# Mixture of experts behind attention: tokens chosen ahead of the last shared expert, twelve pair slots for the weights, two scatters under way

## The chip, the cores and the metric

The kernel is one launch on one core of a Trainium2 chip. The metric is the device time of that launch in microseconds. The kernel before took 1569.04 us in the median of 3 runs (1566.18 to 1572.91).

## The reference

The input x is 8 batches of 512 tokens with 256 features, all in float32. In short:

```python
x = x + layernorm(attention(layernorm(x)))     # 16 query heads of 128 in 4 groups, causal, softmax
h = layernorm(x)                               # 4096 tokens x 256
scores = softmax(h @ gate_w.T)                 # 64 experts
topk_w, topk_idx = top_k(scores, 6)
# each expert takes the first 64 tokens that chose it (CAP = 64), in order of the token's number;
# for these: d = (silu(t @ w_gate[e]) * (t @ w_up[e])) @ w_down[e]     # 256 -> 176 -> 256
# y[token] = sum over its experts of topk_w * d
y = y + (silu(h @ sh_gate.T) * (h @ sh_up.T)) @ sh_down.T              # shared expert, 352 wide
x = x + layernorm(y)
```

An expert never has more than 64 tokens, and most of the 4096 x 6 choices are dropped. What an expert puts out is added to the rows of its tokens; two experts can have a token in common.

## The kernel before, in words

Everything lives in one program with five instruction streams (SP for plain DMAs, POOL, ACT, DVE, PE), tied by semaphores that are written out by hand. The order of the work is fixed in Python loops; nothing is scheduled at run time.

Attention goes head by head through 128 steps (8 batches x 16 heads). Each batch's output projection, norms, router and shared expert are fitted between the heads of the next batch by a table of places. For the last batch there is no next one, so its rest is done after attention: `turn_y`, `turn_x2`, `route`, `turn_mask`, then six pieces of the shared expert's gate and up (`gate_up`, three column blocks for each of two lanes of 256 tokens) and two of its down projection (`shared_down`). In a piece of `gate_up` ACT makes the tanh (L910), DVE two products (L1238, L1248), ACT the high part (L917) and POOL the low part (`gate_low`, L1486); a lane's product buffer is used again only when POOL has read it.

Each expert's tokens are found as the 64 largest of a row of keys (4096 minus the token's number, or zero). `pick` (L1220) takes eight of them with a MAX8 and a MATCH_REPLACE8 on DVE; for the last batch its eight calls stand between and behind the pieces of `gate_up` (L1353 to 1362). DVE then makes two tables, of tokens to gather and of rows to scatter to, PE turns them (L763, L764), and DVE copies them as integers (L1380). An empty place gathers a row of zeros and scatters to a row set apart for it.

The experts are worked off in 32 pairs: expert 2j in partitions 0 to 63, expert 2j+1 in 64 to 127. For a pair, POOL gathers 128 rows of 320 values (the token's features and its 64 router weights) with an indirect DMA (`gather`, L1545), PE turns them (`expert_turn`, L767), ACT copies, PE multiplies with gate and up (`expert_in`, L777), ACT makes the tanh, DVE the products (`expert_act`, L1383), PE turns (`activations_turn`), ACT copies, PE multiplies with down (`expert_out`, L800), ACT copies to a buffer `dsum` (L1015), and POOL adds the 128 rows to the table `ffn_sums` in HBM with an indirect DMA that accumulates (`scatter`, L1552). The table has two copies: the first expert of a pair adds to copy 0, which also has the shared expert's rows, the second to copy 1. So no row is named twice in one scatter. Rows can be named in two scatters that follow each other, so scatter j waits until scatter j-1 has landed (L1554). There are 5 buffers for gathered rows (NX) and 3 for `dsum` (ND). POOL's order is: four gathers, then for each pair gather j+4 and scatter j.

SP loads the weights expert by expert, three DMAs of 176 KB each (L456), into 16 slots; the first 16 experts are loaded at the end of attention and beside the last batch's rest, the others each when the pair that had the slot has been through `expert_out`. Between them SP reads back the rows that the last residual adds (`fx`, L478). When the last scatter has landed (L503), SP loads both copies of the table (`load_sums`), POOL and DVE add them, DVE and POOL make mean and variance, ACT normalises, DVE adds `fx`, SP stores.

The waits around the scatter:

```python
def scatter(j):                                  # L1552
    if j:
        pool.wait_ge(dma_s, 16 * j)              # scatter j-1 has landed
    ...
    pool.wait_ge(d_made, j + 1)
```

Of the kernel before, what the change touches and what calls it, by code (L numbers as in the profile page):

```python
# [14 lines left out]
P = 128  # L15
TOP_K = 6
CAP = 64
# [13 lines left out]
def build(nc, x, wq, bqT, wkv, bkvT, wo, gwT, w_gate, w_up, w_down, sgT, suT, sdT, consts, out):  # L31
# [6 lines left out]
    NE, _, F = w_gate.shape  # L38
# [7 lines left out]
    TRASH = CAP  # L46
# [14 lines left out]
    sum_rows = [sums[a * SUMROWS:a * SUMROWS + NT, :].rearrange("(b i p) e -> b p i e", p=P, i=TT)  # L61
                for a in range(2)]
    out_rows = out.rearrange("b (i p) e -> b p i e", p=P)

    with ExitStack() as ctx:
# [30 lines left out]
        slot_row = place("slot_row", [P, CAP], F32)  # L96
# [52 lines left out]
        NW = 16  # L149
        w_gu, w_dn, w_where = [], [], []  # L150
        for s in range(NW):
            w_gu.append(place(f"w_gu{s}", [P, 2, 2 * F], F32))
            w_dn.append(place(f"w_dn{s}", [P, 2, E], F32))
            w_where.append(at[0])
        assert at[0] <= weights_end

        at[0] = heads_at
        NX, ND = 5, 3
# [5 lines left out]
        atr = [place(f"atr{i}", [P, 2, P], F32) for i in range(2)]  # L164
        dsum = [place(f"dsum{i}", [P, E], F32) for i in range(ND)]
        tok2 = place("tok2", [P, 2 * CAP], F32)
        sct2 = place("sct2", [P, 2 * CAP], F32)
        empty = place("empty", [P, CAP], F32)
# [9 lines left out]
        at[0] = after_experts  # L178
        NFB = 4
# [4 lines left out]
        fb = [place(f"fb{i}", [P, TT, E], F32) for i in range(2)]  # L184
        assert at[0] <= end_at, (at[0], end_at)
        at[0] = work_at
        fb += [place(f"fb{i}", [P, TT, E], F32) for i in range(2, NFB)]
        fx = [place(f"fx{b}", [P, TT, E], F32) for b in range(NB)]

# [5 lines left out]
        def plain(ap):  # L195
# [9 lines left out]
        dma_s, dma_out = sem("dma_s"), sem("dma_out")  # L205
# [21 lines left out]
                                    "act_turned", "atr_made", "down_in", "d_made"))  # L227
        sum_pool, sum_dve, bias_made, final_normed, final_made = (
# [85 lines left out]

        def lane_of(b, k):
            return k if b == LAST else 0
# [68 lines left out]
        def sync_program(sp):  # L385
# [12 lines left out]
            for t, n in ((ident, P), (pe_t, T), (key_row, HT), (slot_row, CAP), (causal[:, T - P:T], P)):  # L398
# [3 lines left out]
            sp.dma_start(bkv_s[:], bkvT).then_inc(dma_const, 16)  # L402
            for n in range(6):
                load_piece(n)
# [22 lines left out]
            def store_ffn(b, k):  # L427
                _, _, taken, u = use("sd", b, k)
                sp.wait_ge(taken, u + 1)
                sp.dma_start(sum_rows[0][b, :, 2 * k:2 * k + 2, :],  # L430
# [40 lines left out]
            for e in range(NW):  # L471
                if w_where[e] > wkv_end:
                    sp.wait_ge(out_in, N)
                load_expert(e)
            sp.wait_ge(out_in, N)
            sp.wait_ge(values_in, 4 * N)
            for b in range(LAST):
                sp.dma_start(fx[b][:], x2_rows[b]).then_inc(dma_x2in, 16)  # L478
# [5 lines left out]
            for j in range(NP):  # L484
                for u in range(2):
                    if 2 * j + u + NW < NE:
                        load_expert(2 * j + u + NW)
                if j == 1:
# [1176 lines left out]
```

## Time and profile before

| | |
|---|---|
| median of 3 runs | 1569.04 us |
| profiled execution | 1569.09 us, span 1567.3 us, mean granted clock share of TensorE 0.939 |
| busy | PE 1369.7 us (87%), DVE 1089.5 (70%), ACT 840.9 (54%), POOL 814.3 (52%) |
| DMA | 95.78 MB, 61 GB/s over the span; 88722 packets of the plain queue, 6144 of POOL's |
| L1559, scatter issue on POOL | 32 times, 1575 ns each, 97.1 us of idle time before them |

The profile's page has the span in 40 slices of 39.2 us. PE shows nines in slices 3 to 31 and between 0 and 7 after that; the DMA row is near zero in the middle and 4 to 9 from slice 32 on. The change concerns that end: from about 1240 us, where the last heads run and the first weights are loaded, to 1567 us. In the rows below, times are microseconds from the span's start unless marked otherwise, and a line number is that of the kernel before.

### The profile page before, as it was taken

Reading aid. Unit: us, or ns where it says so; the run is one execution under the profiler, and the core shown is the slowest. Engines: PE = TensorE matmul, PEld = TensorE weight load, DVE = VectorE, ACT = ScalarE, POOL = GpSimd, SP = SyncE. Lnnn points to the kernel's source line nnn. Section 1 sums busy time; section 2 is a strip of 40 time slices with the busy share of each in tenths; the row PEclk is TensorE's granted clock in tenths of the full one; section 3 lists DMA queues with packets and bytes.
Section 4 is the critical chain, followed back from the end, with each engine's and each line's share of the span. In section 5 each row is a group of like instructions: output and inputs, shape, how many; then the busy total and the mean of one; then the engine's idle time right before and its main releaser. Section 6 shows DMA issues by size and latency. Waiting matters only on the chain.

```text
span 1567.3 us, 25800 instructions
## 1 busy us (share of the span) xinstructions
PE 1369.7 (87%) x8322; PEld 1168.2 (75%) x8322; DVE 1089.5 (70%) x3524; ACT 840.9 (54%) x2267; POOL 814.3 (52%) x1309
## 2 busy tenths in 40 slices
PE   3899999999999999999999999999999936676710
PEld 3788889888988898889888988898889835333310
DVE  4867686888688868887888688868886855111117
ACT  4666665665566566666666666666665611222204
POOL 2555564556454645464556455645564512344446
PEclk9899999999999999999999999999999967788865
DMA  7100000100000010001000100010000481999765
GB/s 271 46 1 1 14 15 9 37 15 15 22 28 10 14 38 22 1 15 38 21 1 15 38 21 1 15 38 21 1 14 25 110 240 52 237 241 239 165 168 170
DMA packets 94997, 95.78 MB, mean 61 GB/s; under 512 B 6065, under 2 KB 87314, under 8 KB 94866
## 3 DMA queue, kind: packets, MB, share of 16 engines
q1 hardware_dynamic: 88722, 84.70, 17.9%
q0 software_dynamic: 6144, 9.44, 3.1%
q8 instruction: 69, 1.13, 0.3%
q14 instruction: 62, 0.51, 0.1%
HBM read 67.78 MB, written 26.35 MB: 60 GB/s over the span
## 4 chain that ended last, share of the span: by engine, by line
PE 59%; DVE 18%; POOL 7%; DMA 6%; issue 6%; ACT 3%; SPq 0%; POOLq 0%; ACTq 0%; DVEq 0%
PE bank_s L520 14%; PE bank_t L520 13%; PE bank_o L520 10%; PE bank_y L520 9%; PE bank_f L520 5%; DMA ffn_sums<-dsum,idx_s 4%; PE bank_s L600 3%; DVE rows L1081 2%; PE bank_t L600 2%; DVE stat L1060 2%; DVE prob L1148 2%; DVE q_sum L1125 2%; PE bank_f L600 1%; DVE o_l L1166 1%; DVE pt_l L1161 1%
## 5 line engine op out<-in xcount | busy, mean ns | idle before, releaser
L1474 POOL TENSOR_TENSOR prob<-prob,rinv 128x512 f32<-128x512 f32 (+3 forms) x512 | 366.6, 724 | 206.3 <-DVE rinv L1155 204.3
L858 ACT ACTIVATE prob<-prob,negmax 128x512 f32<-128x512 f32 (+3 forms) x512 | 285.5, 558 | 87.8 <-DVE negmax L1148 87.1
L1461 POOL TENSOR_TENSOR q_l<-q_sum,q_h 128x128 fp32r<-128x128 f32 (+1 forms) x256 | 185.5, 745 | 144.4 <-ACT q_h L838 143.2
L520 PE MATMUL bank_o<-pt_h,v_h 128*128 128x128 f32 (+3 forms) x512 | 169.4, 331 | 0.0
L520 PE MATMUL bank_o<-pt_h,v_l 128*128 128x128 f32 (+3 forms) x512 | 165.0, 322 | 0.0
L520 PE MATMUL bank_o<-pt_l,v_h 128*128 128x128 f32 (+3 forms) x512 | 164.0, 320 | 0.0
L867 ACT ACTIVATE pt_h<-bank_s 128x128 fp32r<-128x128 f32 (+3 forms) x214 | 92.8, 434 | 78.2 <-PE bank_s L600 59.6
L838 ACT ACTIVATE q_h<-q_sum 128x512 fp32r<-128x512 f32 x128 | 80.3, 627 | 89.4 <-DVE q_sum L1125 89.4
L1148 DVE CUSTOM_DVE_ANT_0 prob<-bank_t,causal 128x384 f32<-128x384 f32 (+3 forms) x226 | 110.3, 488 | 24.0 <-PE bank_t L520 23.2
L1148 DVE CUSTOM_DVE_ANT_0 prob<-bank_s,causal 128x512 f32<-128x512 f32 (+3 forms) x217 | 107.7, 496 | 25.8 <-PE bank_s L520 24.8
L520 PE MATMUL bank_y<-o_h,wo_h 128*128 128x512 f32 x256 | 112.7, 440 | 5.5 <-DVE o_l L1166 5.5
L1155 DVE RECIPROCAL rinv<-rsum 128x1 f32<-128x1 f32 x512 | 80.4, 157 | 45.8 <-ACT prob L858 44.4
L1395 DVE SCALAR_TENSOR_TENSOR ex<-ex,bank_s 128x176 f32<-128x176 f32 x32 | 10.8, 337 | 142.5 <-ACT ex L1008 142.5
L1166 DVE SCALAR_TENSOR_TENSOR o_l<-bank_o,bkv_s,o_h 128x512 fp32r<-128x512 f32 x128 | 94.9, 741 | 21.2 <-ACT o_h L874 21.1
L1161 DVE TENSOR_TENSOR pt_l<-bank_s,pt_h 128x128 fp32r<-128x128 f32 (+3 forms) x214 | 103.4, 483 | 1.2
L520 PEld LDWEIGHTS bank_o<-pt_l,v_h 128*128 128x128 f32 x512 | 96.8, 189 | 5.9
L520 PEld LDWEIGHTS bank_o<-pt_h,v_h 128*128 128x128 f32 x512 | 96.4, 188 | 6.4
L600 PE MATMUL bank_s<-ident,prob 128*128 128x128 f32 x538 | 95.9, 277 | 5.9 <-POOL prob L1474 3.9
L520 PEld LDWEIGHTS bank_o<-pt_h,v_l 128*128 128x128 f32 x512 | 96.6, 189 | 6.0
L520 PE MATMUL bank_y<-o_h,wo_l 128*128 128x512 f32 x256 | 101.0, 394 | 0.0
L520 PE MATMUL bank_y<-o_l,wo_h 128*128 128x512 f32 x256 | 100.9, 394 | 0.0
L1559 POOL DMA_INDIRECT ffn_sums<-dsum,idx_s x32 | 50.4, 1575 | 97.1 <-DMA ffn_sums<-dsum,idx_s 86.3
(352 smaller groups left out, 4235.8 us busy)
## 6 DMA issues: line engine op xcount, KB each, us to landing
w_gu<-in_w_gate SPq DMA_DIRECT2D x64, 176.0 KB
w_gu<-in_w_up SPq DMA_DIRECT2D x64, 176.0 KB
w_dn<-in_w_down SPq DMA_DIRECT2D x64, 176.0 KB
xio<-in_x SPq DMA_DIRECT2D x16, 512.0 KB, 4.0
token_table<-rows SPq DMA_DIRECT2D x8, 640.0 KB, 3.7
ffn_sums<-keys SPq DMA_DIRECT2D x4, 1024.0 KB
x_rows<-xio SPq DMA_DIRECT2D x8, 512.0 KB, 2.9
ffn_sums<-ytr SPq DMA_DIRECT2D x16, 256.0 KB, 2.1
```

The lines of the kernel that those rows point to most:

```text
L520: return pe.matmul(o, l, r, start=start, stop=stop, skip_group_check=True)
L600: last = pe.transpose(bk[:, (i - j) * P:(i - j + 1) * P], prob[:, r, tri[i] + j * P:tri[i] + (j + 1) * P], ident[:])
L838: act.activation(h_, q_sum[:], ACT.Copy).then_inc(pos_high, 1)
L858: act.activation(p_, p_, ACT.Exp, bias=negmax[:, r, i:i + 1], scale=-1.0, accum_out=rsum[:, r, i:i + 1]).then_inc(exp_made, 1)
L867: act.activation(pt_h[:, inv[j]:inv[j + 1]], bk[:, 0:(TT - j) * P], ACT.Copy).then_inc(pt_high, 1)
L1148: dve.tensor_tensor_reduce(out=prob[:, r, tri[i]:tri[i + 1]], in0=bk[:, 0:w], in1=causal[:, T - w:T], scale=-1.0, scalar=BIG, op0=ALU.add, ...
L1155: dve.reciprocal(rinv[:, r, i:i + 1], rsum[:, r, i:i + 1]).then_inc(row_inv, 1)
L1161: dve.tensor_tensor(l_, bk[:, 0:(TT - j) * P], plain(h_), ALU.subtract).then_inc(taken, 1)
L1166: dve.scalar_tensor_tensor(out=o_l[:], in0=bank["o"][:], scalar=bkv_s[:, 2 * g + 1:2 * g + 2], in1=plain(o_h[:]), op0=ALU.add, op1=ALU.sub ...
L1461: pool.tensor_tensor(l_[:, cols], q_sum[:, cols], plain(h_)[:, cols], ALU.subtract).then_inc(pos_low, 1)
L1474: pool.tensor_tensor(p_, p_, rinv[:, r, i:i + 1].to_broadcast([P, (i + 1) * P]), ALU.mult).then_inc(prob_made, 1)
L1559: pool.indirect_dma_start(sums, bass.IndirectOffsetOnAxis(idx_s[:, j:j + 1].bitcast(U32), 0), dsum[j % ND][:], None, compute_op=ALU.add).t ...
```

## The change

- **Tokens chosen first.** All eight picks of the last batch, the two tables and their turn come ahead of DVE's `gate_up`. PE does five pieces of `gate_up`, the transposes (now three, into bank o), then the sixth. POOL issues seven gathers ahead of its six `gate_low`.
- **Slots.** Weights lie in HBM by pairs, gate and up side by side, so that a partition's share of a pair is one piece (5632 B for gate and up, 4096 B for down), loaded by two DMAs. There are 12 pair slots (24 experts); four of them lie where attention kept its keys and values. `fx` is no longer loaded there ahead of the experts but after the last weights, when pair 23 has been through `expert_out`.
- **Buffers.** 8 for gathered rows, 4 for `dsum`.
- **Two scatters.** Pairs take the two copies of the table in turn: pair j adds to copy j mod 2, with both its experts, and scatter j waits for scatter j-2. Since both experts of a pair now add to one copy, their common tokens are joined: PE writes the first expert's token numbers along the columns (a matmul of 64 columns), DVE compares them with the second's (`same`), PE adds the second expert's matching rows to the first's in PSUM (`add_second`), and DVE sends the second expert's row to a place set apart if it had a match (`targets`). ACT copies the second half of `dsum` ahead of that matmul and the first half after it (`first_out`), which stands one pair later in the order.
- **Last stage.** A partition takes four rows that follow each other (4 KB pieces) instead of every 128th, and there is a second buffer for each batch, so no load waits for one.

The core of the diff:

```diff
-    TRASH = CAP
+    TRASH = 2 * CAP
...
-        NW = 16
+        NW, NWA = 12, 8
...
-        NX, ND = 5, 3
+        NX, ND = 8, 4
...
-            def load_expert(e):
-                s = e % NW
-                if e >= NW:
-                    sp.wait_ge(down_in, (e - NW) // 2 + 1)
-                for k, w in enumerate((w_gate, w_up)):
-                    sp.dma_start(w_gu[s][:, :, k * F:(k + 1) * F],
-                                 w[e].rearrange("(p c) f -> p c f", c=2)).then_inc(dma_w[s], 16)
-                sp.dma_start(w_dn[s][0:F2, :, :],
-                             w_down[e].rearrange("(p c) h -> p c h", c=2)).then_inc(dma_w[s], 16)
+            def load_pair(j):
+                s = j % NW
+                if j >= NW:
+                    sp.wait_ge(down_in, j - NW + 1)
+                sp.dma_start(w_gu[s][:], w_in[j]).then_inc(dma_w[s], 16)
+                sp.dma_start(w_dn[s][0:F2], w_out[j]).then_inc(dma_w[s], 16)
...
+            for j in range(NWA, NW):
+                load_pair(j)
             store_x2(LAST)
             store_rows(LAST)
             store_ffn(LAST, 0)
             store_ffn(LAST, 1)
...
+            for j in range(NW, NP):
+                load_pair(j)
+
+            sp.wait_ge(dma_x2, 16 * NB)
+            sp.wait_ge(down_in, NP // NW * NW)
+            for b in range(NB):
+                sp.dma_start(fx[b][:], x2_runs[b]).then_inc(dma_x2in, 16)
...
+            gates = [(k, n) for n in range(NF) for k in range(2)]
+            for k, n in gates[:EARLY]:
+                gate_up(LAST, k, n)
+            pe.wait_ge(slots_made, 1)
+            pe.transpose(bank["o"][:, 0:NE], tok2[0:NE, :], ident[0:NE, 0:NE])
+            pe.transpose(bank["o"][:, NE:2 * NE], sct2[0:NE, :], ident[0:NE, 0:NE])
+            pe.transpose(bank["o"][:, 2 * NE:3 * NE], aside2[0:NE, :], ident[0:NE, 0:NE]).then_inc(slots_turned, 1)
+            for k, n in gates[EARLY:]:
+                gate_up(LAST, k, n)
             for k in range(2):
                 shared_down(LAST, k)
...
+                mm(bk[CAP:2 * CAP, 2 * F:2 * F + CAP], ident[0:NE, 2 * j:2 * j + 1].to_broadcast([NE, CAP]),
+                   tok2[0:NE, 0:CAP], start=True, stop=True)
...
+            def add_second(j):
+
+                pe.wait_ge(same_made, j + 1)
+                pe.wait_ge(second_made, j + 1)
+                mm(bank[f"t{j % 2}"][0:CAP, 0:E], same[j % 2][CAP:2 * CAP, :], dsum[j % ND][CAP:2 * CAP, :], stop=True
+                   ).then_inc(same_in, 1)
...
             for j in range(NP):
                 if j + 2 < NP:
                     expert_turn(j + 2)
+                if j:
+                    add_second(j - 1)
                 activations_turn(j)
                 if j + 1 < NP:
                     expert_in(j + 1)
                 expert_out(j)
+            add_second(NP - 1)
...
             def expert_out(j):
                 if j >= ND:
-                    act.wait_ge(dma_s, 16 * (j - ND + 1))
+                    act.wait_ge(dma_s[j % 2], 16 * ((j - ND) // 2 + 1))
                 act.wait_ge(down_in, j + 1)
-                act.activation(dsum[j % ND][:], bank[f"t{j % 2}"][:, 0:E], ACT.Copy).then_inc(d_made, 1)
+                act.activation(dsum[j % ND][CAP:2 * CAP, :], bank[f"t{j % 2}"][CAP:2 * CAP, 0:E], ACT.Copy
+                               ).then_inc(second_made, 1)
+
+            def first_out(j):
+                act.wait_ge(same_in, j + 1)
+                act.activation(dsum[j % ND][0:CAP, :], bank[f"t{j % 2}"][0:CAP, 0:E], ACT.Copy).then_inc(d_made, 1)
...
+            def targets(j):
+
+
+                r, at_ = j % 2, slice(CAP, 2 * CAP)
+                done(dve.tensor_reduce(twice[r][at_, :], same[r][at_, :], AX, ALU.max))
+                dve.scalar_tensor_tensor(out=idx_s[at_, j:j + 1], in0=twice[r][at_, :], scalar=second[at_, 2, j:j + 1],
+                                         in1=second[at_, 1, j:j + 1], op0=ALU.mult, op1=ALU.add
+                                         ).then_inc(target_made, 1)
...
+                dve.tensor_scalar(same[r][at_, :], bk[at_, 2 * F:2 * F + CAP], second[at_, 0, j:j + 1], None,
+                                  ALU.is_equal).then_inc(same_made, 1)
+                dve.wait_ge(same_made, j + 1)
...
             def scatter(j):
-                if j:
-                    pool.wait_ge(dma_s, 16 * j)
-                else:
+                if j > 1:
+
+                    pool.wait_ge(dma_s[j % 2], 16 * (j // 2))
+                elif not j:
                     pool.wait_ge(dma_ffn[0], 16 * NB)
                     pool.wait_ge(dma_ffn[1], 16 * NB)
+                pool.wait_ge(target_made, j + 1)
                 pool.wait_ge(d_made, j + 1)
...
             for j in range(NX - 1):
                 gather(j)
+            for n in range(NF):
+                for k in range(2):
+                    gate_low(LAST, k, n)
```

## Rows read from the trace of the kernel before

**Rows 1.** Stages: us, length, busy us (instructions) by engine, clock share, DMA share, GB/s
```profile
1318.80:1333.50 14.70, 10.29 (x40) 4.61 (x42) 2.18 (x10) 3.20 (x9) 4.99 (x5) 0.65 0.20 58
1333.50:1472.00 138.50, 95.35 (x473) 49.71 (x470) 21.89 (x93) 32.45 (x93) 58.98 (x46) 0.78 0.93 239
1472.00:1509.50 37.50, 19.30 (x132) 10.92 (x128) 6.13 (x26) 8.98 (x26) 18.05 (x13) 0.86 0.36 57
1509.50:1567.30 57.80, 0.00 (x0) 0.00 (x0) 32.37 (x92) 16.16 (x32) 32.11 (x64) 0.50 0.66 218
```

**Rows 2.** Waits from 1333.5 to 1472 us: total us, times, longest
```profile
POOL ffn_sums L1559 <- DMA ffn_sums<-dsum,idx_s: 67.4, 21, 5.5
...
PE bank_y L774 <- DMA xg<-token_table,idx_g: 43.1, 21, 4.1
```

**Rows 3.** Timeline of POOL: scatters 0, 1, 23 and 31 (start, length)
```profile
1333.52 1.62 POOL L1559 DMA_INDIRECT ffn_sums<-dsum,idx_s  x1 [8.52 <-ACT dsum L1019]
...
1338.76 1.58 POOL L1559 DMA_INDIRECT ffn_sums<-dsum,idx_s  x1 [2.32 <-ACT dsum L1019]
...
1472.01 1.57 POOL L1559 DMA_INDIRECT ffn_sums<-dsum,idx_s  x1 [2.75 <-DMA ffn_sums<-dsum,idx_s]
...
1505.81 1.55 POOL L1559 DMA_INDIRECT ffn_sums<-dsum,idx_s  x1 [2.46 <-DMA ffn_sums<-dsum,idx_s]
```

**Rows 4.** DMA queues from 1318 to 1506 us: packets, MB, share
```profile
q1 hardware_dynamic: 31664, 26.75, 51.4%
q0 software_dynamic: 6000, 9.31, 25.7%
```

**Rows 5.** Timeline of DVE: end of the masks, picks 5 and 8, slot arithmetic
```profile
1293.05 0.42 DVE L1217 TENSOR_SCALAR rows<-rows,router_soft 128x64 f32<-128x64 f32 x2
...
1310.20 0.75 DVE L1227 MAX8 first<-keys 64x8 f32<-64x576 f32 x1
...
1315.10 0.75 DVE L1227 MAX8 first<-keys 64x8 f32<-64x576 f32 x1
...
1316.32 0.21 DVE L1368 SCALAR_TENSOR_TENSOR empty<-keys,slot_row 64x64 f32<-64x64 f32 x1
```

**Rows 6.** Timeline of POOL: the first two gathers
```profile
1318.79 1.19 POOL L1548 DMA_INDIRECT xg<-token_table,idx_g  x1 [7.26 <-DVE idx_s L1380]
1320.28 0.98 POOL L1548 DMA_INDIRECT xg<-token_table,idx_g  x1 [0.30 <-issue]
```

**Rows 7.** Timeline of the shared expert's end and the first expert turn
```profile
1302.12 0.42 DVE L1238 SCALAR_TENSOR_TENSOR sig<-sig,bank_f 128x256 f32<-128x256 f32 x1
...
1303.74 0.42 DVE L1238 SCALAR_TENSOR_TENSOR sig_b<-sig_b,bank_s 128x256 f32<-128x256 f32 x1 [0.75 <-ACT sig_b L910]
...
1309.19 0.72 POOL L1486 TENSOR_TENSOR a_l<-act,a_h 96x256 fp32r<-96x256 f32 x1 [3.32 <-ACT a_h L917]
...
1310.06 0.55 PE L520 MATMUL bank_t<-sd_h,a_h 128*128 128x256 f32 x1 [6.77 <-POOL a_l L1486]
...
1316.30 0.28 PE L520 MATMUL bank_f<-sd_h,ab_l 96*128 96x256 f32 x1
...
1321.90 0.70 PE L774 MATMUL bank_y<-ident,xg 128*128 128x128 f32 x2 [4.23 <-DMA xg<-token_table,idx_g]
```

**Rows 8.** Timeline of PE: pairs 2 and 3, gate and up, then down
```profile
1332.86 1.41 PE L520 MATMUL bank_s<-w_gu,xt 128*64 128x352 f32 x8
1334.10 1.08 PE L520 MATMUL bank_t<-w_dn,atr 88*64 88x256 f32 x8
...
1336.02 1.41 PE L520 MATMUL bank_s<-w_gu,xt 128*64 128x352 f32 x8
```

**Rows 9.** DMA from 1243 to 1255, from 1511 to 1530, from 27 to 34
```profile
DMA packets 3430, 2.87 MB, mean 239 GB/s; under 512 B 228, under 2 KB 2973, under 8 KB 3430
...
DMA packets 6592, 6.56 MB, mean 345 GB/s; under 512 B 191, under 2 KB 6592, under 8 KB 6592
...
DMA packets 2615, 2.63 MB, mean 376 GB/s; under 512 B 46, under 2 KB 2615, under 8 KB 2615
```

More of the change, by code:

```diff
@@ L95, in build @@
         key_row = place("key_row", [P, HT], F32)
-        slot_row = place("slot_row", [P, CAP], F32)
+        copy_at = place("copy_at", [P, 2], F32)
         causal = place("causal", [P, T], F32)
@@ L163, in build @@
         ag = [place(f"ag{i}", [P, F], F32) for i in range(2)]
-        atr = [place(f"atr{i}", [P, 2, P], F32) for i in range(2)]
-        dsum = [place(f"dsum{i}", [P, E], F32) for i in range(ND)]
         tok2 = place("tok2", [P, 2 * CAP], F32)
         sct2 = place("sct2", [P, 2 * CAP], F32)
-        empty = place("empty", [P, CAP], F32)
+        aside2 = place("aside2", [P, 2 * CAP], F32)
+        second = place("second", [P, 3, NP], F32)
+        same = [place(f"same{i}", [P, CAP], F32) for i in range(2)]
+        twice = [place(f"twice{i}", [P, 1], F32) for i in range(2)]
         idx_g = place("idx_g", [P, NP], I32)
@@ L204, in build @@
         dma_g = [sem(f"dma_g{i}") for i in range(NX)]
-        dma_s, dma_out = sem("dma_s"), sem("dma_out")
+        dma_s, dma_out = [sem(f"dma_s{i}") for i in range(2)], sem("dma_out")
         dma_f = [sem(f"dma_f{b}") for b in range(NB)]
@@ L1026, in scalar_program @@
                     expert_turn(j + 2)
+                if j:
+                    first_out(j - 1)
                 activations_turn(j)
@@ L1352, in vector_program @@
                     step(LAST, k)
-            r = 0
+            for r in range(CAP // 8):
+                pick(LAST, r)
+            key = keys[0:NE, 0:CAP]
+            slot = key_row[0:NE, 0:2 * CAP]
+            for u in range(2):
+                at_ = slice(u * CAP, (u + 1) * CAP)
+                dve.tensor_scalar(tok2[0:NE, at_], key, -1.0, float(NT), ALU.mult, ALU.add)
+                last = dve.scalar_tensor_tensor(out=aside2[0:NE, at_], in0=key, scalar=0.0, in1=slot[:, at_],
+                                                op0=ALU.is_equal, op1=ALU.mult)
+            done(last)
+            done(dve.scalar_tensor_tensor(out=sct2[0:NE, :], in0=tok2[0:NE, :], scalar=copy_at[0:NE, 0:1],
+                                          in1=aside2[0:NE, :], op0=ALU.add, op1=ALU.subtract))
+            dve.scalar_tensor_tensor(out=aside2[0:NE, :], in0=sct2[0:NE, :], scalar=copy_at[0:NE, 1:2],
+                                     in1=slot, op0=ALU.subtract, op1=ALU.add).then_inc(slots_made, 1)
+            dve.wait_ge(slots_turned, 1)
+            turned = bank["o"][:, 0:3 * NE].rearrange("p (k j two) -> p k j two", k=3, two=2)
+            for u in range(2):
+                at_ = slice(u * CAP, (u + 1) * CAP)
+                dve.tensor_copy(idx_g[at_, :], turned[at_, 0, :, u])
+            dve.tensor_copy(idx_s[0:CAP, :], turned[0:CAP, 1, :, 0])
+            at_ = slice(CAP, 2 * CAP)
+            dve.tensor_copy(second[at_, 0:2, :], turned[at_, 0:2, :, 1])
+            dve.tensor_scalar(second[at_, 2, :], turned[at_, 2, :, 1], -1.0, None, ALU.mult).then_inc(index_made, 1)
+            dve.wait_ge(index_made, 1)
             for n in range(NF):
@@ L1536, in gpsimd_program @@
                 newton(nw, TT, r)
-            for n in range(NF):
-                for k in range(2):
-                    gate_low(LAST, k, n)
             pool.wait_ge(index_made, 1)
```

148 lines of the change are left out of this document (62 added, 86 removed).

## The prediction

> **What bounds the kernel now.** I read the stage table first. Attention runs on a full TensorE until about 1263 us and the change leaves it alone, so only what follows counts. The expert loop, from the first scatter at 1333.5 us to the last, landed at 1509.5 us, is the largest piece of the tail. In it no compute engine is full: PE is busy 95.4 of the first 138.5 us, while the DMA engines show a share of 0.93 [rows 1]. The table of waits then says what the order of work waits for: POOL sits in front of its scatters for 67.4 us until the scatter before has landed, and PE sits 43.1 us for gathered tokens, which POOL issues behind those scatters [rows 2]. So I read POOL's own timeline. A scatter waits for the one before it, so the distance from scatter to scatter is one scatter's way through POOL and DMA. While weights stream it is (1472.01 - 1338.76) / 22 = 6.06 us; for the last eight steps, with hardly any weights left, (1505.81 - 1472.01) / 8 = 4.2 us [rows 3]. From first to last: (1505.81 - 1333.52) / 31 = 5.56 us a pair. The last landing is 3.7 us after its issue (1509.5).
>
> The DMA table tells why it is 6.06 and not 4.2. Between 1318 and 1506 us the weight queue moved 26.75 MB in 51.4% of 188 us, which is 96.6 us, or 277 GB/s; the gathers and scatters took 25.7%, 48.3 us, 1.5 us a pair [rows 4]. A pair's weights are 6 x 176 KB = 1.08 MB, 3.9 us, so a pair in the loaded part asks 5.4 us of the engines, out of 6.06. The chain is bound by the scatter's latency, but the bytes stand close behind it. This is the main point of the forecast: letting two scatters run does not halve the time, it hands the loop to the next bound.
>
> **The change, step by step.** All against the profiled execution, 1569.09 us with a span of 1567.3 (the 1.8 us around it stay); it is 0.05 us above the median of the runs.
>
> Tokens chosen first. Router and mask end on DVE at 1293.5 [rows 5]. Eight picks come now in a row; three steps took 1315.10 - 1310.20 = 4.90, so 1.63 each [rows 5], 8 x 1.63 = 13.0 with the copy that ends the last. The slot arithmetic is four small operations on 64 rows of 64 and two of 128, near the 0.21 us row [rows 5], 1.2 us; three transposes instead of two and five copies, for which I take 1.8 us (from 1316.32 to the first gather the kernel before needed 2.5, with two more slot operations, two transposes and four copies in it [rows 5, 6]). That is about 1309.4 for the first gather, 9.4 us sooner than 1318.79 [rows 6]. It buys nothing by itself, since POOL now issues seven gathers before the six subtractions of the shared expert (gate_low), which stand behind them in its queue: 1.19 + 6 x 1.28 = 8.9 (a gather takes 0.98 and 0.3 to the next) [rows 6], so POOL is free for the first gate_low at 1318.3. Who waits for it: DVE may fill the gate buffer of a lane again only when a_low is made, so DVE and ACT do the first two gates and then stop. After 1318.3 four gates are left at 1.62 us each, the pitch of the serial chain DVE, DVE, ACT, ACT (1302.12 to 1303.74) [rows 7], of which lane 0 needs three: 1318.3 + 0.8 + 3 x 1.62 = 1324.0 with the last subtraction of 0.73 us nearly inside it. So the down projection begins near 1324 against 1310.06 [rows 7]; it takes 6.5 us as before (1310.06 to 1316.58), to 1330.5. The experts can then begin at once, as seven pairs of tokens are there: 1330.5 against 1321.90 [rows 7], 8.6 us late. From there to the first scatter the old kernel needed 11.6 us at a clock share of 0.65 [rows 1]; the new one waits for no gather in between but has one more PE step and ACT copy, and TensorE comes straight from work: I take 9 (between 8 and 11.6), first scatter 1339.4 against 1333.52. **Term 1: +5.8 us** (bounds +1 if DVE's picks and POOL overlap better than I follow, +9).
>
> The cadence. Lower bounds first.
> - PE. Pairs 2 and 3 ran with nothing to wait for at full speed: 1332.86 to 1336.02 is 3.16 us a pair [rows 8]. The change adds a matmul of 64 columns (under 0.1 us) and the add of the common tokens, 256 columns in one group where w_dn has four of them in 1.08 us [rows 8], so 0.27. That makes 3.5. On the dependent side, DVE gets one compare before the gate product, 0.2 us near [rows 5], and the turn of the activations waits for it about as long as PE is busy with the added matmul; no further cost. ACT's second copy and DVE's max and index operation, all near 0.2 to 0.4 us, lie beside PE. If PE falls to half clock, as in the first pairs, twice 3.5.
> - POOL: scatter 1.57, gather 0.98 and 0.3 behind each [rows 3, 6], 3.2 us a pair.
> - Scatter latency: with two under way it is 6.06 / 2 = 3.0 if two do not slow each other, 6.06 if they share so badly that nothing is won.
> - Bytes. Twelve pairs are loaded ahead instead of eight (four of them in the place of the x2 rows fx, which are read at the end), so 20 pairs, 21.6 MB, are left, and 4.2 MB of fx. Pieces grow from 704 B to 5632 B for gate and up and from 2048 B to 4096 B for down. Two rates of plain queues bound this: weights alone in the old layout 239 GB/s, whole rows of 1 KB read for the last stage 345 GB/s, and a pure store of 376 GB/s [rows 9]. I take 345, the nearest row for reads in straight pieces: 62.7 us of weights, 12.2 of fx, 48.3 of gathers and scatters, less 3.5 for the seven gathers already done (0.5 each, a third of the 1.5 of a pair, estimated): 119.7. The old loop ran at a share of 0.93 at best, so 128 us from about 1336.5, when the first slot is given back: 1464.5. By 376 GB/s it is 1456, by 239 it is 1500.
>
> The bytes are thus a little later than PE (31 x 3.5 = 109). Spread over 31 steps from 1339.4 to 1464.5 less 3.7 for the landing, the bytes ask 3.9 us a pair. I take 3.9: 31 x 3.9 = 120.9 against 172.3. **Term 2: -51.4 us** (bounds: 3.5 gives -63.8; 5.1, from 239 GB/s, gives -14.2).
>
> The last stage begins when both kinds of scatters have landed, 57.8 us from the end [rows 1]. Its loads now take 4 KB pieces and no longer wait for buffers, but after the first four batches (4.2 MB) DVE, POOL and ACT take turns. 4.2 MB at 345 is 12.2 us, at 376 11.2. **Term 3: -1 us** (0 to -3). The fx loads stand ahead of these in SP's queue; they are issued when pair 23 is through its down product, eight pairs or 31 us before the end, and hide under the loop if the weights are done by then; if not, up to 5 us come back here.
>
> Loading ahead with 12 slots costs nothing before 1330: x2 and the token rows are stored behind 4.3 MB instead of 3.7, 2 us later at most, and the first gather at 1309 has 10 us left. Sum: 5.8 - 51.4 - 1 = -46.6, 1569.1 - 46.6 = **1522.5 us**.
>
> Of the Trainium skill one rule speaks against this. DMA: Bandwidth & Descriptors, Queues, rings and completion order, says that an engine serves its queues in turn and drains a whole packet of several descriptors before it goes on to the other queue; longer weight pieces would then make each turn of the weights longer, and the gathers and scatters would wait behind them. No view here shows turns. What it would make of the time is the first rival.
>
> **Rivals.**
> (a) The loop stays bound by DMA at 4.8 to 5.7 us a pair while weights stream. A long weight piece keeps an engine 8 times as long as a 704 B one, about 0.26 us at 345 / 16 GB/s, and an engine has 8 of them per load, 2.1 us. If the gather and the scatter of a pair each wait for one load, that is 4.2 + 1.5 = 5.7; if for half of one, 3.6 to 4.8 with PE. For it: the scatter took 6.06 loaded and 4.2 unloaded already with short pieces [rows 3]. Against: total engine time falls. With 20 pairs at 5.2 and 11 at 4.1: 149, term 2 is -23, the time 1569 + 5.8 - 23 - 1 = 1551; at the light end, 4.6 then 3.6, 131.6, 1533.
> (b) PE alone sets the pace, 3.5 us, because large pieces run at 376 GB/s or more and the share goes to 1: 1569.1 + 4 - 63.8 - 1.5 = 1508. For it: slots are deep, 12 pairs. Against: the share of 0.93.
> (c) Slower. Two scatters with read and write back, a gather, and 5.6 KB pieces in between: if each of a pair's gather and scatter packets on an engine waits for two such pieces, 12 packets (6000 over 16 engines and 62 to 64 transfers is 6 a transfer [rows 4]) x 0.52 + 1.5 = 7.7 us a pair while 20 pairs load, then 4.1: 154 + 45 = 199, term 2 is +27, the time 1601. It decides from a mean cadence of 5.4 us, where term 2 no longer pays term 1. Against it: packets of both queues ran beside each other before at 1.5 us a pair.
> (d) The change does nothing, since scatters are still serialised by the POOL queue: 3.2 us of POOL against 6.06 excludes it; I give it no chance of its own.
>
> **Chances.** Forecast (1512 to 1531) 0.50, (a) 0.25, (b) 0.20, (c) 0.05. The range reaches into (a) and (b): 1504 to 1555. A measurement of this kernel tells no less than 0.5% from no change. Faster by more than that 0.94, within 0.02, slower 0.04.
>
> **What would show it.** Right: first gather near 1309, the down projection of the last shared expert near 1324, first expert turn near 1330; scatters 3.9 us apart with POOL no longer waiting for the one before; weight queue above 320 GB/s; DMA share above 0.9 until about 1455; span from last landing 57 us. Scatter distance of 3.5 with PE full means (b); scatters 5 apart with POOL or ACT waiting for a landing means (a). Wrong altogether: a half clock on TensorE through the loop, which would make PE the bound at 5 us or more, or experts that wait for weights.

## The result, and the profile after

The changed kernel takes 1530.61 us (median of 4 runs, 1528.46 to 1534.34); the kernel before took 1570.64 us beside it (4 runs, 1566.18 to 1572.91). The ratio is 0.9763 [0.9737, 0.9789]. The profiled execution took 1528.5 us, with a span of 1526.7 against 1567.3: 40.6 us shorter, where 46.6 were forecast.

The stages of the kernel after, with the same columns as [rows 1]: from the first gather to the first expert turn, from there to the first scatter (these two windows overlap by 0.3 us), up to scatter 24, the rest of the loop, the last stage.
```profile
1307.70:1329.70 22.00, 10.26 (x51) 9.94 (x52) 4.97 (x14) 4.50 (x13) 12.15 (x14) 0.60 0.25 72
1329.40:1339.20 9.80, 8.02 (x51) 4.44 (x51) 3.52 (x14) 4.07 (x11) 0.00 (x0) 1.00 0.21 64
1339.20:1444.00 104.80, 99.59 (x611) 54.44 (x609) 43.95 (x175) 46.18 (x126) 61.53 (x48) 1.00 1.01 298
1444.00:1471.00 27.00, 19.07 (x114) 9.71 (x110) 8.50 (x33) 8.96 (x25) 12.43 (x8) 0.89 0.50 92
1471.00:1526.70 55.70, 0.00 (x0) 0.00 (x0) 33.52 (x92) 16.16 (x32) 32.20 (x64) 0.50 0.57 226
```
In the loaded part of the loop TensorE is now busy for 99.59 of 104.80 us at a granted clock of 1.00, its upper level (before: 95.35 of 138.50 at 0.78), and the DMA engines show a share of 1.01. Two columns are full at once, so this view can't say which of them sets the pace.

POOL's timeline, with the rows that answer to [rows 3] and [rows 6]: first gather, the first and the fifth of the six subtractions of the shared expert (the fifth is the last of lane 0, for which the down projection waits), scatters 0, 1, 5, 24 and 31.
```profile
1307.69 1.19 POOL L1595 DMA_INDIRECT xg<-token_table,idx_g  x1 [27.33 <-DVE second L1408]
...
1316.40 0.74 POOL L1536 TENSOR_TENSOR a_l<-act,a_h 128x256 fp32r<-128x256 f32 x1
...
1321.44 0.72 POOL L1536 TENSOR_TENSOR a_l<-act,a_h 96x256 fp32r<-96x256 f32 x1 [0.89 <-ACT a_h L938]
...
1339.21 1.62 POOL L1608 DMA_INDIRECT ffn_sums<-dsum,idx_s  x1 [14.31 <-ACT dsum L1045]
1343.24 1.58 POOL L1608 DMA_INDIRECT ffn_sums<-dsum,idx_s  x1 [1.10 <-ACT dsum L1045]
...
1359.91 1.57 POOL L1608 DMA_INDIRECT ffn_sums<-dsum,idx_s  x1 [1.53 <-DMA ffn_sums<-dsum,idx_s]
...
1444.00 1.58 POOL L1608 DMA_INDIRECT ffn_sums<-dsum,idx_s  x1 [1.23 <-DMA ffn_sums<-dsum,idx_s]
...
1467.23 1.55 POOL L1608 DMA_INDIRECT ffn_sums<-dsum,idx_s  x1 [2.13 <-ACT dsum L1045]
```
Scatters stand (1467.23 - 1339.21) / 31 = 4.13 us apart, against 5.56. Scatters 5 to 24 are 4.43 apart, and some still wait for a landing.

Waits from 1339.2 to 1444 us (total us, times, longest), which answer to [rows 2]:
```profile
POOL ffn_sums L1608 <- DMA ffn_sums<-dsum,idx_s: 27.5, 18, 3.3
POOL ffn_sums L1608 <- ACT dsum L1045: 21.5, 6, 14.3
...
ACT dsum L1040 <- DMA ffn_sums<-dsum,idx_s: 2.7, 3, 1.4
```
POOL still waits 27.5 us for landings (before 67.4), but PE's 43.1 us for gathered tokens are gone. Who is paced by whom is seen where PE starts its products. PE's timeline of the kernel after: the down products of pairs 0 and 30, and between them one whole pair.
```profile
1335.72 1.08 PE L529 MATMUL bank_t<-w_dn,atr 88*64 88x256 f32 x8
...
1408.52 1.41 PE L529 MATMUL bank_s<-w_gu,xt 128*64 128x352 f32 x8
1409.76 1.08 PE L529 MATMUL bank_t<-w_dn,atr 88*64 88x256 f32 x8
1410.77 0.50 PE L784 MATMUL bank_y<-ident,xg 128*128 128x128 f32 x2
1411.46 0.61 PE L529 MATMUL bank_t<-dsum,same 64*64 64x256 f32 x2 [0.19 <-ACT dsum L1040]
1412.00 0.46 PE L809 MATMUL bank_f<-ident,ag 128*88 128x128 f32 x2
1412.39 0.32 PE L529 MATMUL bank_s<-tok,ident 64*64 64x64 f32 x2
1412.65 0.82 PE L529 MATMUL bank_s<-w_gu,xt 128*64 128x352 f32 x4
...
1460.05 1.08 PE L529 MATMUL bank_t<-w_dn,atr 88*64 88x256 f32 x8
```
Thirty down products lie in (1460.05 - 1335.72) = 124.33 us, 4.14 each, and from product to product it is 4.07 for the first four and 4.13 then, but for one of 4.90. The scatters are late in the middle and catch up by the end (scatter 24 is 6 us behind what 4.13 a pair would give, scatter 31 is not). The four `dsum` buffers keep nearly all of that from PE: ACT, which empties PE's banks into them, waited for a landing for 2.7 us in all. So by the trace PE's own sequence sets the loop.

The DMA queues from 1318 to 1470 us, which answer to [rows 4]:
```profile
q1 hardware_dynamic: 6556, 26.35, 52.3%
q0 software_dynamic: 5716, 8.22, 27.9%
```
26.35 MB in 52.3% of 152 us is 331 GB/s, against 277 (345 were taken for the weights). And PE's rows that answer to [rows 7]: the down projection of the last shared expert and the first expert turn.
```profile
1322.31 0.55 PE L529 MATMUL bank_t<-sd_h,a_h 128*128 128x256 f32 x1 [11.08 <-POOL a_l L1536]
...
1329.45 0.65 PE L784 MATMUL bank_y<-ident,xg 128*128 128x128 f32 x4
```

### The profile page after: what moved, and what is told of

Its sections match the earlier page's. It is cut to its first block and busy times, and to the rows that moved or that the text cites. A ratio compares the mean times of both kernels' runs of the same rounds, so it can differ in the third digit from the quotient of the medians.

```text
span 1526.7 us, 26086 instructions
## 1 busy us (share of the span) xinstructions
PE 1374.1 (90%) x8451; PEld 1175.1 (77%) x8451; DVE 1117.0 (73%) x3622; ACT 855.1 (56%) x2299; POOL 814.1 (53%) x1309
## 5 line engine op out<-in xcount | busy, mean ns | idle before, releaser
L888 ACT ACTIVATE pt_h<-bank_t 128x128 fp32r<-128x128 f32 (+3 forms) x173 | 74.4, 430 | 48.9 <-PE bank_t L609 34.0
L879 ACT ACTIVATION_READ_ACCUMULATOR prob<-prob,negmax 128x1 f32 x512 | 97.2, 190 | 0.0
```

The costliest lines, as they stand in the source:

```text
L879: act.activation(p_, p_, ACT.Exp, bias=negmax[:, r, i:i + 1], scale=-1.0, accum_out=rsum[:, r, i:i + 1]).then_inc(exp_made, 1)
L888: act.activation(pt_h[:, inv[j]:inv[j + 1]], bk[:, 0:(TT - j) * P], ACT.Copy).then_inc(pt_high, 1)
```

## The experiments

The question left was what holds the loop at 4.13 us a pair: PE's sequence, the landings and bytes, or the shared rows that now meet in scatters under way together; and which part of the change brings the 40 us. "Pace" below is the mean distance of the 32 scatters. The kernel before took 1568.23 us (median) beside no_join, no_refill, one_scatter and low_first, 1567.31 beside own_rows, small_pieces, before_pairs and low_first_add_late, 1565.86 beside no_join_small, one_small, low_late_small and half_pieces. Lines of the diffs are those of the kernel after, unless another is named.

### no_join: the joining left out
```diff
-                mm(bk[CAP:2 * CAP, 2 * F:2 * F + CAP], ident[0:NE, 2 * j:2 * j + 1].to_broadcast([NE, CAP]),
-                   tok2[0:NE, 0:CAP], start=True, stop=True)
...
-                if j:
-                    add_second(j - 1)
...
-                act.activation(dsum[j % ND][CAP:2 * CAP, :], bank[f"t{j % 2}"][CAP:2 * CAP, 0:E], ACT.Copy
-                               ).then_inc(second_made, 1)
+                act.activation(dsum[j % ND][:], bank[f"t{j % 2}"][:, 0:E], ACT.Copy).then_inc(d_made, 1)
...
+            dve.tensor_tensor(idx_s[at_, :], second[at_, 1, :], second[at_, 2, :], ALU.add).then_inc(index_made, 1)
...
-                dve.tensor_scalar(same[r][at_, :], bk[at_, 2 * F:2 * F + CAP], second[at_, 0, j:j + 1], None,
-                                  ALU.is_equal).then_inc(same_made, 1)
```


> The changed kernel without the joining of a pair's common tokens: no matmul of 64 columns, no compare, no add_second, no max and index operation, one ACT copy instead of two; every row of the second expert goes to the rows set apart, so that part of the sum is missing. Traffic on the DMA engines stays. Theory 1 (the loop is paced by TensorE's own order, 4.13 us a pair, of which the added 0.26 + 0.54 us and a wait of 0.18 are nearly 1): scatters 3.2 to 3.5 us apart, time down by 20 to 28 us, 1502 to 1510 us. Theory 2 (the loop is paced by bytes and landings; the DMA share is 0.98 to 1.05): scatters stay 4.0 to 4.1 apart, TensorE gets gaps, 1525 to 1530 us.

Measured: 1525.83 us, 0.9723 [0.9673, 0.9774], pace 4.13, which looks as if nothing had happened. PE's down products show two phases that happen to give the same mean.
```profile
1361.92 1.08 PE L529 MATMUL bank_t<-w_dn,atr 88*64 88x256 f32 x8
...
1367.50 0.88 PE L529 MATMUL bank_t<-w_dn,atr 88*64 88x256 f32 x6 [2.23 <-ACT atr L1027]
```
Up to 1361.92 they are 3.16 us apart, as in [rows 8]; then 5.58, and uneven from there. Scatters 5 to 24 are (1446.46 - 1356.50) / 19 = 4.73 apart. Its waits from 1340 to 1465 us say why:
```profile
ACT dsum L1034 <- DMA ffn_sums<-dsum,idx_s: 53.8, 19, 5.1
POOL ffn_sums L1590 <- DMA ffn_sums<-dsum,idx_s: 45.8, 23, 4.3
```
ACT waits for `dsum` buffers, that is for landings: all four are taken. So the joining is what sets PE's 4.13, and a second bound, the landings at 4.73, shows once PE runs ahead. The time and the pace are those of theory 2, but the first phase shows what theory 1 says of PE: each theory has half of it.

### no_refill: pairs 12 to 31 not loaded
```diff
-            for j in range(NW, NP):
-                load_pair(j)
...
-                pe.wait_ge(dma_w[j % NW], 32 * (j // NW + 1))
+                pe.wait_ge(dma_w[j % NW], 32)
```


> The changed kernel without the loads of pairs 12 to 31: these pairs multiply with the weights that lie in their slots, so their outputs are wrong; 21.6 MB are not moved in the loop. Theory 1: TensorE still needs 4.13 us a pair, scatters stay 4.13 apart and only their landings get shorter (8.3 us to about 4), the time stays within 3 us of the changed kernel's, 1526 to 1531. Theory 2: scatters come 3.5 us apart or closer, time down by 20 us or more.

Measured: 1526.73 us, 0.9741 [0.9702, 0.978], pace 4.09; scatters 5 to 24 are 4.13 apart. Its scatters 0 and 31, and its only large wait of POOL from 1340 to 1465 us:
```profile
1339.13 1.62 POOL L1605 DMA_INDIRECT ffn_sums<-dsum,idx_s  x1 [14.32 <-ACT dsum L1042]
...
1465.96 1.55 POOL L1605 DMA_INDIRECT ffn_sums<-dsum,idx_s  x1 [1.72 <-ACT dsum L1042]
```
```profile
POOL ffn_sums L1605 <- ACT dsum L1042: 57.2, 30, 14.3
```
With the DMA engines at a share of 0.42 (1360 to 1430 us) and scatters that land in 3.8 us (median), the pace stays. This is the plainest proof that PE's sequence sets it, not the landings and not the bytes on which the forecast's 3.9 rested.

### one_scatter and one_small: the wait for the scatter before put back
```diff
-                if j > 1:
-
-                    pool.wait_ge(dma_s[j % 2], 16 * (j // 2))
-                elif not j:
+                if j:
+                    pool.wait_ge(dma_s[(j - 1) % 2], 16 * ((j - 1) // 2 + 1))
+                else:
```
one_small has, besides, the short pieces of small_pieces below.

> The changed kernel with one wait put back: scatter j waits until scatter j-1 has landed; all else as changed. Theory 1 says that the second scatter under way is what took the landing out of the chain: a landing alone under load should be 5 to 6 us, the distance of scatters 5 to 6 us, the time 1560 to 1585 us, that is nearly all of the 40 us given back. Theory 3 (the gain comes from the large weight pieces, which shorten a landing): distance 4.2 to 4.5 us, the time 1530 to 1542.

> small_pieces with the wait put back: scatter j waits until scatter j-1 has landed. Against small_pieces (1526 us) it prices the second scatter under way alone, without the length of the pieces. Scatters ran 5.56 us apart in the kernel before and 5.77 with one scatter and large pieces; I expect 5.4 to 5.6 and 1562 to 1572 us. If short pieces did most of the work, it would be under 5.0 and under 1555 us.

Measured: one_scatter 1576.74 us, 1.0048 [1.0027, 1.0069], pace 5.77. one_small 1574.34 us, 1.0054 [1.0037, 1.007], pace 5.55, which is the old kernel's 5.56. The two scatters of one_small that answer to [rows 3]:
```profile
1339.09 1.62 POOL L1610 DMA_INDIRECT ffn_sums<-dsum,idx_s  x1 [13.87 <-ACT dsum L1048]
...
1511.12 1.55 POOL L1610 DMA_INDIRECT ffn_sums<-dsum,idx_s  x1 [2.55 <-DMA ffn_sums<-dsum,idx_s]
```
All else that the change brings is in these kernels, and they are slightly slower than the kernel before. Without the second scatter under way nothing of the gain is left: 5.55 against the 4.10 of small_pieces is 31 x 1.45 = 45 us. Whether the second scatter would give as much without the twelve slots and the added buffers was not tested.

### low_first: the subtractions ahead of the seven gathers
```diff
+            for n in range(NF):
+                for k in range(2):
+                    gate_low(LAST, k, n)
             pool.wait_ge(index_made, 1)
...
-            for n in range(NF):
-                for k in range(2):
-                    gate_low(LAST, k, n)
             for j in range(NP):
```


> The changed kernel with POOL's six gate_low ahead of its seven gathers. In the changed kernel the first scatter came at 1339.2 us, 5.7 later than before, which the prediction put down to the subtractions behind the gathers. If that is so, the last shared expert's down projection begins near 1316 instead of 1322.3, the first scatter near 1333.5 to 1334.5, and the time falls by 4.5 to 6 us, to about 1524. If the delay has another cause (the DVE order, TensorE's clock), the first scatter stays within 1 us of 1339.2 and the time with it.

Measured: 1524.62 us, 0.9732 [0.9689, 0.9775]. PE's first expert turn:
```profile
1322.23 0.64 PE L784 MATMUL bank_y<-ident,xg 128*128 128x128 f32 x4
```
It is 7.2 us sooner than 1329.45, and so is the first scatter (1332.00); that is term 1's price for standing behind seven gathers. But the last scatter comes only 4.4 us sooner (1462.83), the span ends 3.1 sooner. Scatters 5 to 24 are 4.56 apart, and ACT waits 4.4 us for buffers. So 2.8 us are taken back. In the trace two waits for a landing reach PE, 0.4 and 1.4 us beyond its usual 0.2; behind the longer one the granted clock was 0.67 (1414.3 to 1419.5 us), and gate and up and down took 2.12 and 1.80 us instead of 1.24 and 1.01. The kernel after loses 0.8 us of this kind itself.

### own_rows: as no_join, second experts to copies of the table of their own
```diff
-    sums = nc.dram_tensor("ffn_sums", [2 * SUMROWS, E], F32, kind="Internal").ap()
+    sums = nc.dram_tensor("ffn_sums", [4 * SUMROWS, E], F32, kind="Internal").ap()
...
-            zero_left, per, n0 = 2 * SUMROWS - NT, ZERO_PER, NT
+            zero_left, per, n0 = 4 * SUMROWS - NT, ZERO_PER, NT
...
+            dve.tensor_scalar(idx_s[at_, :], turned[at_, 1, :, 1], float(2 * SUMROWS), None, ALU.add).then_inc(index_made, 1)
```


> The changed kernel without the joining, as in no_join, but every second expert adds to a third and fourth copy of the table instead of 64 rows set apart; these copies are cleared in the first stage and never read, so the second experts are missing from the output. no_join had TensorE light and still 4.1 us a pair, with all second halves on the same 64 rows. If those hot rows were its brake, scatters come 3.4 to 3.8 us apart here and the time is 1505 to 1517 us (theory 1 whole: TensorE's order alone holds the changed kernel). If the engines' bytes and landings are the next bound, close behind TensorE, the distance stays 3.9 to 4.3 and the time 1520 to 1530.

Measured: 1547.83 us, 0.9859 [0.9823, 0.9895], pace 4.11, scatters 5 to 24 again 4.73 apart. So rows that second experts share in no_join are not what holds its landings up. The time can't be compared: clearing the larger table delays the start. The first 60 us of own_rows and then of the kernel after, columns as in [rows 1]:
```profile
0.00:60.00 60.00, 20.37 (x77) 15.17 (x77) 23.69 (x49) 16.52 (x24) 11.48 (x25) 0.80 0.89 301
```
```profile
0.00:60.00 60.00, 32.34 (x131) 25.43 (x132) 36.26 (x89) 28.63 (x58) 20.53 (x37) 0.83 0.61 208
```
PE has done 12 us less by 60 us, and another 12 us less by 100 us (27.88 of 40 us busy, against 40.00); 12 stores of 1 MB instead of 4 stand in the queue among its inputs.

### small_pieces and half_pieces: how long a piece of the weights is
The layout in HBM and the 12 slots stay. small_pieces loads a pair in six DMAs with pieces of 704 and 2048 B as before the change, half_pieces in four with 2816 and 2048 B.
```diff
-                sp.dma_start(w_gu[s][:], w_in[j]).then_inc(dma_w[s], 16)
-                sp.dma_start(w_dn[s][0:F2], w_out[j]).then_inc(dma_w[s], 16)
+                for u in range(2):
+                    for k in range(2):
+                        cols = slice(k * F, (k + 1) * F)
+                        sp.dma_start(w_gu[s][:, u, :, cols], w_in[j][:, u, :, cols]).then_inc(dma_w[s], 16)
+                    sp.dma_start(w_dn[s][0:F2, u], w_out[j][:, u]).then_inc(dma_w[s], 16)
```


> The changed kernel with each pair's weights loaded by six DMAs in pieces of 704 B (gate, up) and 2048 B (down) as before, into the same 12 slots. By the rows of before (239 to 277 GB/s for such pieces) 20 pairs take 78 to 90 us instead of about 65, so the bytes ask for 4.4 to 4.9 us a pair: the time is 1540 to 1555 us. If the engines are not the limit near 4.1 us (TensorE alone is), it stays at 1528 to 1533.

> The changed kernel with pieces of 2816 B (gate and up) and 2048 B (down), four DMAs a pair: between the large pieces (5632 and 4096 B: 4.43 us from scatter 5 to scatter 24, gathers land in 7.8 us) and the small ones (704 and 2048 B: 4.13 us, 6.2 us). If the length of a piece sets how long gathers and scatters wait, landings and distance lie between the two, 4.2 to 4.4 and about 7 us. If it is another trait of the large loads (two DMAs issued at once, alignment), they equal one of the ends.

Measured: small_pieces 1526.32 us, 0.9739 [0.9717, 0.976], pace 4.10, not slower than the kernel after: of its two cases the second came, that of TensorE alone as the limit. half_pieces 1527.91 us, 0.9756 [0.9729, 0.9784], pace 4.11; scatters 5 to 24 are 4.13 apart in both, so the 4.2 to 4.4 expected of half_pieces missed. The queues from 1360 to 1430 us, in the kernel after and then in small_pieces:
```profile
q1 hardware_dynamic: 3537, 15.73, 70.4%
```
```profile
q1 hardware_dynamic: 16688, 14.04, 72.4%
```
Long pieces do move bytes faster, 15.73 MB in 70.4% of 70 us, 319 GB/s, against 277. Yet a gather lands 7.8 us after its issue (median, 1335 to 1465 us), with short pieces 6.2. POOL's waits for landings in small_pieces from 1345 to 1432 us:
```profile
POOL ffn_sums L1611 <- ACT dsum L1048: 18.8, 15, 1.3
POOL ffn_sums L1611 <- DMA ffn_sums<-dsum,idx_s: 7.6, 6, 1.3
```
In the same stretch POOL waits for landings for 25.0 us in the kernel after and 19.6 in half_pieces, so these waits grow with the length of a piece: 7.6, 19.6, 25.0. The rate is bought with latency, and while PE sets the pace neither is seen in the time.

### before_pairs: the kernel before with the long pieces alone
```diff
-        NW = 16
+        NW = 8
...
+            def load_pair(j):
+                s = j % NW
+                if j >= NW:
+                    sp.wait_ge(down_in, j - NW + 1)
+                sp.dma_start(w_gu[s][:], w_in[j]).then_inc(dma_w[s], 16)
+                sp.dma_start(w_dn[s][0:F2], w_out[j]).then_inc(dma_w[s], 16)
```


> The kernel before with one part of the change: weights by pairs in large pieces, two DMAs a pair, into 8 pair slots. Scatters still wait for the one before. If a landing is shortened by what the engines have to do (bytes), the distance falls from 5.56 to about 5.0 us and the time to 1550 to 1556. If a landing is held up by the length of the pieces ahead of it, as the rule on turns between queues would have it, the distance stays at 5.5 to 5.9 (in one_scatter it was 5.76 with large pieces) and the time at 1565 to 1580.

Measured: 1575.86 us, 1.0055 [1.0038, 1.0072]. From first (1329.41) to last scatter it is 181.5 us, against 172.3 in [rows 3], and 5.85 a pair: where one landing follows another, a landing's length goes into the pace. One row of its timeline against scatter 31 in [rows 3]:
```profile
1510.89 1.55 POOL L1553 DMA_INDIRECT ffn_sums<-dsum,idx_s  x1 [2.43 <-DMA ffn_sums<-dsum,idx_s]
```

### no_join_small: short pieces, and the joining left out
Its edit is those of no_join and small_pieces together.

> no_join (joining left out, second experts' rows all go to the rows set apart) with the weights in pieces of 704 B and 2048 B. With large pieces the distance of scatters while weights stream was 4.73 us although TensorE had work for 3.2 to 3.5 only. Theory 4 (what stood behind TensorE in the changed kernel is the turn of the gathers and scatters behind long weight pieces, not the bytes): distance 3.4 to 3.9 us in that stretch, time 1500 to 1515 us. Theory 2 (the bytes): 4.3 us or more as with large pieces, time 1522 or more.

Measured: 1515.78 us, 0.9675 [0.9646, 0.9703], pace 3.81, also for scatters 5 to 24, where no_join had 4.73. Its window from 1360 to 1430 us and the waits in it:
```profile
1360.00:1430.00 70.00, 57.63 (x363) 31.15 (x362) 17.09 (x74) 22.83 (x75) 46.17 (x36) 0.98 1.06 277
```
```profile
ACT dsum L1037 <- DMA ffn_sums<-dsum,idx_s: 33.0, 14, 3.3
...
POOL ffn_sums L1593 <- DMA ffn_sums<-dsum,idx_s: 16.0, 15, 1.7
```
PE is busy for 57.6 of 70 us, the DMA engines show a share of 1.06, and ACT waits for buffers. So with PE relieved the landings are the bound, 3.8 us a pair with short pieces and 4.7 with long ones, and short pieces are worth 0.9 us a pair here and nothing under PE. How much of the 3.8 is bytes and how much the time of two landings was not separated: no run left out the joining and the loads together.

### low_first_add_late and low_late_small: other orders
PE turns the activations before it adds the common tokens; ACT's copy of the first half moves with it. low_late_small has that, low_first and small_pieces.
```diff
+                activations_turn(j)
                 if j:
                     add_second(j - 1)
-                activations_turn(j)
```


> low_first and besides PE's add_second behind the turn of the activations instead of ahead of it (ACT's order likewise), which is to hide the 0.18 us that PE waits for ACT's copy. If TensorE's order is all that counts, 31 x 0.1 to 0.18 = 3 to 5.6 us less than low_first, 1519 to 1522 us. If the DMA engines are level with it, under 2 us.

> The three edits that each took something off, together: gate_low ahead of the gathers, add_second behind the turn of the activations, weights in small pieces. First scatter near 1331.5, distance 4.0 to 4.1 us held by TensorE throughout, so 1331.5 + 31 x 4.05 + 3.7 + 55.7 + 1.8 = 1518 us; theory 2 (bytes level with TensorE) would leave it at 1523 as low_first_add_late.

Measured: low_first_add_late 1523.11 us, 0.974 [0.9701, 0.9779], pace 4.19; the order alone is worth nothing that can be told. low_late_small 1518.76 us (5 runs, 1517.69 to 1521.69), 0.9702 [0.9677, 0.9726], pace 4.00. It beats both kernels: first scatter at 1333.26, and the landings no longer take back what the earlier start gives. A pair on PE in it:
```profile
1407.97 0.43 PE L812 MATMUL bank_o<-ident,ag 128*88 128x128 f32 x2 [0.36 <-DVE ag L1450]
1408.33 0.43 PE L532 MATMUL bank_t<-dsum,same 64*64 64x256 f32 x1
1408.34 0.32 PE L532 MATMUL bank_s<-tok,ident 64*64 64x64 f32 x2
1408.60 0.38 PE L532 MATMUL bank_t<-dsum,same 64*64 64x256 f32 x1
1408.90 1.41 PE L532 MATMUL bank_s<-w_gu,xt 128*64 128x352 f32 x8
1410.14 1.08 PE L532 MATMUL bank_t<-w_dn,atr 88*64 88x256 f32 x8
1411.15 0.50 PE L787 MATMUL bank_y<-ident,xg 128*128 128x128 f32 x2
1412.02 0.43 PE L812 MATMUL bank_f<-ident,ag 128*88 128x128 f32 x2 [0.36 <-DVE ag L1450]
```
From turn to turn it is 4.05. The wait of 0.19 for ACT's copy has gone, and one of 0.36 for DVE's product has come: PE waits in either order, for ACT or for DVE. What makes the pace 0.08 shorter all the same is that the add and the matmul of 64 columns now stand side by side: they start 0.01 us apart (1408.33 and 1408.34) and need 0.57 together (to 1408.90), where in the kernel after, with the turn of the activations between them, they need 0.54 and 0.26.

## Why the prediction was right, step by step

**What bounds the loop, and that the change moves it to the next bound**: right. Scatters one after the other cost 5.56 us a pair, and putting that wait back restores 5.55 (one_small). Which bound comes next was wrong: the prediction took the bytes, and it is PE. So two of its signs did not come: scatters 3.9 apart with POOL no longer waiting for the one before (4.13, and 27.5 us of waits for landings), and a DMA share above 0.9 until about 1455 (1.01 until 1444, then 0.67 to 1455).

**Term 1**, forecast +5.8, measured 1339.21 - 1333.52 = +5.7. Its stations: first gather 1307.7 (forecast 1309.4), POOL free at 1316.4 (1318.3), down projection 1322.3 (1324), first expert turn 1329.45 (1330.5), 9.8 us more to the first scatter (9). low_first shows that it is the place of the subtractions in POOL's queue, worth 7.2 us.

**Term 2**, forecast -51.4, measured 128.0 - 172.3 = -44.3: here lie 7.1 us, more than the whole miss of 6.0. The step that failed is the lower bound "That makes 3.5" for PE, which measures 4.13; being too low, it let the bytes' 3.9 pass for the later bound. From the pair shown above: gate and up 1.24, down 1.01, turn of the tokens 0.50 and 0.19 of wait, add 0.54, turn of the activations 0.39, matmul of 64 columns 0.26, together 4.13. Against 3.16 that is +0.14 (the turn with its wait was 0.55 in no_join), +0.54 (forecast 0.27), +0.26 (under 0.1) and 0.03. The add was sized as a quarter of the down product's 1.08. Two rows of single instructions (duration ns min/median/max, first and last start), from the down product and the add of that pair, say what was wrong with it:
```profile
L529 PE MATMUL bank_t<-w_dn,atr x8: 377/379/422, 1409.8 to 1410.5; 88*64 88x256 f32 x8
```
```profile
L529 PE MATMUL bank_t<-dsum,same x2: 376/386/397, 1411.5 to 1411.7; 64*64 64x256 f32 x2
```
A 256-column matmul is two instructions here. The down product's eight, of 379 ns each, need 1.01 us to the next step, 0.13 each, so several lie over each other; the add's two of 386 ns need 0.54, 0.27 each. In the trace the eight start two by two: 0.01 to 0.06 us between the two, and 0.22 from one two to the next. They belong to two experts, in different halves of the output; so do the add and the matmul of 64 columns that stand side by side in low_late_small. The two of the add write the same half and start 0.24 apart. So what overlaps here are matmuls into different halves. No run tested that alone; the add also takes 64 rows and 64 columns where the turns beside it take 128 rows and 88 or 128 columns (64*64, 128*88, 128*128 in the rows), and what that change costs was not separated.

**The bytes**, forecast 3.9: not the bound here (no_refill). What stands next asks 3.8 with short pieces (no_join_small), but 4.7 with the long ones that this kernel has (no_join), so the term was too low for this kernel; 345 GB/s were taken for the weights, and 319 to 331 were measured. That the time fell inside the forecast's range is in part luck: the value 3.9 came from the wrong bound, and the right one was undersized by 0.6. One of the bounds is also off in its sum: by 376 GB/s the terms give 1458, not 1456; nothing rests on it.

**The clock**, named as what could overthrow it: it went the other way. A PE that no longer waits for tokens was granted 1.00 in the loop instead of 0.78.

**Term 3**, forecast -1, measured 55.7 - 57.8 = -2.1. The first row that the last stage adds shows it waiting for the first load alone:
```profile
1475.78 2.03 POOL L1624 TENSOR_TENSOR fa<-fa,fb 128x768 f32<-128x768 f32 x1 [7.00 <-DMA fb<-ffn_sums]
```
All loads are issued within 8.5 us, from 1471.0 to 1479.5, where the old ones took 18.4 us; of these SP waited for a buffer for 1.5 us only, and single issues took longer (up to 2.1 us, against 1.1). The three terms give 5.7 - 44.3 - 2.1 = -40.7, which is the difference of the spans but for rounding.

**The rivals.** (a), landings held up by long pieces: the effect is there, in the landing of a gather (7.8 against 6.2 us), in before_pairs (+9.2 us over the loop) and in no_join (4.73 against 3.81), near its light end (4.6 while weights stream), and under PE's sequence it costs nothing. That agrees in direction with the Trainium skill, DMA: Bandwidth & Descriptors, Queues, rings and completion order, by which an engine drains a queue's packet before it turns to the next queue; no view here shows turns, and the 5.7 us worked out for it did not come. (b), PE alone sets the pace: true, but at 4.13 and not at 3.5. (c) and (d) are out: pace 4.13, and 45 us when the second scatter is taken away.

## What to carry to other kernels

Before a serialising wait is taken away, size every next bound, and size PE's from the distance between starts in a stretch of the same kind: here a short matmul that stood alone cost twice what its share of a batch of overlapping ones said. Two bounds can give the same number: only a run that takes one of them wholly away (no_refill), or a look at the distances pair by pair (no_join), tells which it is. Longer DMA pieces raised the rate of their own queue and lengthened the landings of the other. Where landings were the bound that cost 0.3 us a pair (before_pairs) and 0.9 (no_join); no run here has a loop in which it paid.

## What the runs showed that was not expected

- A two-instruction fp32 matmul that stands alone takes 0.26 us to the next step with 64 columns and 0.54 with 256; eight of 256 columns over two halves of the output take 1.01.
- Weight pieces of 5632 and 4096 B: 319 GB/s and 7.8 us for a gather to land; of 704 and 2048 B: 277 GB/s and 6.2 us. In pace under PE they are alike (4.13, 4.10), without the join they are 4.13 (uneven, 4.73 in the loaded part) and 3.81.
- 8 MB more of stores for clearing in the queue of the first loads cost 22 us in a kernel whose loop kept its pace (own_rows 1547.83 us, no_join 1525.83; first scatter at 1359.43 and 1335.83).
- The DMA engines' share reads 1.01 to 1.06 in the loaded loop of kernels that PE paces (after, small_pieces). A full share is no proof of a bound.
